# Moving the V products of an attention loop behind the next pair's first two products, with their copies and stores

## The reference, cut to what matters

```python
q = _rope((x @ wq).reshape(B, S, 32, 128)); k = _rope((x @ wk).reshape(B, S, 8, 128)); v = (x @ wv).reshape(B, S, 8, 128)
scores = einsum('bqhgd,bshd->bhgqs', qg, k) * sm_scale      # 64 x 64 per sequence and head, causal
attn = softmax(where(allowed, scores, min))
out = einsum('bhgqs,bshd->bqhgd', attn, v).reshape(B, S, 4096) @ wo
x = x + out
```

## Time and profile before

| | us |
|---|---|
| median of 3 runs | 2655.59 (2655.07 to 2657.83) |
| profiled execution | 2657.21 |
| its span in the trace | 2655.4 |
| PE matmuls busy | 2565.0 |
| DVE, POOL, ACT busy | 1672.6, 1442.6, 997.2 |

### The profile page before, as it was taken

The page is one execution under the profiler, slowest core; times in us unless marked ns, Lnnn a source line. Parts: engine busy times, 40 slices in busy tenths (PEclk is TensorE's granted clock), DMA queues, the critical chain, the costliest instruction groups (busy, mean ns, idle before and its releaser), DMA issues.

```text
span 2655.4 us, 37868 instructions
## 1 busy us (share of the span) xinstructions
PE 2565.0 (97%) x12584; PEld 2105.8 (79%) x12584; DVE 1672.6 (63%) x2357; ACT 997.2 (38%) x2440; POOL 1442.6 (54%) x1102
## 2 busy tenths in 40 slices
PE   8999899999998999999999989999999899999999
PEld 7778788888887788878877868888888678787887
DVE  3244566666776888864514456666677688886452
ACT  2043344444444444441204334444444444444120
POOL 0002777777777877730300277777777787773030
PEclk9999999999999999999999999999999999999999
DMA  3511222222225555413431112222222555541232
GB/s 135 174 61 59 68 84 105 104 88 88 104 88 191 178 171 162 140 36 86 133 128 64 60 58 94 105 98 94 88 104 85 186 182 175 159 139 40 78 103 75
DMA packets 150745, 289.96 MB, mean 109 GB/s; under 512 B 14706, under 2 KB 53746, under 8 KB 150562
## 3 DMA queue, kind: packets, MB, share of 16 engines
q1 hardware_dynamic: 105842, 212.08, 25.0%
q10 hardware_dynamic: 44720, 75.51, 7.7%
HBM read 213.41 MB, written 74.12 MB: 108 GB/s over the span
## 4 chain that ended last, share of the span: by engine, by line
PE 84%; POOL 9%; DVE 2%; ACT 2%; issue 1%; SPq 1%; DMA 0%; ACTq 0%; POOLq 0%; DVEq 0%
PE prod L800 26%; PE prod L802 25%; PE prod L801 25%; PE turned L964 4%; PE turned L989 2%; POOL slot L1806 2%; POOL slot_f L1801 2%; POOL s_f L1801 1%; POOL slot L1734 1%; PE turned L976 1%; POOL slot_f L1729 1%; PE turned L822 1%; ACT slot L1522 1%; PE turned L954 1%; DVE x_row L2237 0%
## 5 line engine op out<-in xcount | busy, mean ns | idle before, releaser
L800 PE MATMUL prod<-c_hi,slot 128*128 128x512 f32 x1280 | 510.3, 399 | 35.5 <-ACT p_sum L1560 21.4
L802 PE MATMUL prod<-c_hi,slot 128*128 128x512 f32 x1280 | 500.6, 391 | 0.0
L801 PE MATMUL prod<-c_lo,slot 128*128 128x512 f32 x1280 | 499.9, 391 | 0.0
L800 PE MATMUL prod<-t_hi,slot 128*128 128x512 f32 x960 | 389.7, 406 | 5.9 <-DVE x_row L2237 4.0
L802 PE MATMUL prod<-t_hi,slot 128*128 128x512 f32 x960 | 376.7, 392 | 0.0
L801 PE MATMUL prod<-t_lo,slot 128*128 128x512 f32 x960 | 375.2, 391 | 0.0
L800 PEld LDWEIGHTS prod<-c_hi,slot 128*128 128x128 f32 x1280 | 240.9, 188 | 98.0 <-issue 44.4
L800 PE MATMUL prod<-x_hi,w_hi 128*128 128x512 f32 x656 | 260.1, 396 | 24.2 <-DVE x_lo L1960 9.6
L802 PEld LDWEIGHTS prod<-c_hi,slot 128*128 128x128 f32 x1280 | 241.0, 188 | 51.5
L801 PEld LDWEIGHTS prod<-c_lo,slot 128*128 128x128 f32 x1280 | 241.3, 189 | 47.0
L1729 POOL TENSOR_TENSOR s_f<-raw,raw 128x512 f32<-128x512 f32 x24 | 30.9, 1286 | 454.8 <-DMA raw<-in_wv 454.8
(11 more groups left out here) (202 smaller groups left out, 4995.2 us busy)
## 6 DMA issues: line engine op xcount, KB each, us to landing
o_scratch<-o_f ACTq DMA_DIRECT2D x32, 1024.0 KB, 4.3
c_lo_f<-o_scratch SPq DMA_DIRECT2D x128, 256.0 KB, 3.1
t_lo_f<-o_scratch SPq DMA_DIRECT2D x96, 256.0 KB, 2.9
raw<-in_tw SPq DMA_DIRECT2D x34, 512.0 KB, 3.5
raw_a<-in_wq SPq DMA_DIRECT2D x32, 512.0 KB, 4.1
raw<-in_wq SPq DMA_DIRECT2D x32, 512.0 KB, 4.2
o_scratch<-o_f ACTq DMA_DIRECT2D x30, 512.0 KB, 2.8
raw<-in_wo SPq DMA_DIRECT2D x32, 384.0 KB, 4.2
```

The source lines that it names most:

```text
L800: pe.matmul(dst, wh, xh, start=start, stop=False, skip_group_check=skip)
L801: pe.matmul(dst, wh, xl, start=False, stop=False, skip_group_check=skip)
L802: return pe.matmul(dst, wl, xh, start=False, stop=stop, skip_group_check=skip)
```

## The change

V of a couple's first unit moves from position 6 to 7 (before P1 of the next pair, right ahead of the turn of the second unit's probabilities), V of the second unit from 8 to 9 (before P2 instead of P6; in Q01 pairs right ahead of the first turn of v). On ACT the store of the first unit follows into the next pair, behind `take_p(spill)`, and the store of the second unit stands behind the cast for P6 instead of the cast for P1. The tables for the first slot are changed in the same sense. The number of instructions is the same on every engine; POOL, DVE and SP keep their lists.

```diff
-PV_AT = (6, 8)
+PV_AT = (7, 9)
...
-                TAIL = {(0, P1): [(turn_p, 5)], (0, P6): [(pv, 5), (score, 6)], (0, P7): [(score, 7)],
+                TAIL = {(0, P1): [(pv, 4), (turn_p, 5)], (0, P6): [(score, 6)], (0, P2): [(pv, 5)], (0, P7): [(score, 7)],
...
                     if spill is not None:
                         take_p(B, spill)
+                        o_store(B, spill - 1)
...
-                    if spill is not None:
-                        o_store(B, spill)
                     if host is not None:
                         exp(B, host)
                     if not last:
@@ -1471,6 +1470,8 @@
                     else:
                         w_hi_b(0, P6)
                         o_hi(0, P1)
+                    if spill is not None:
+                        o_store(B, spill)
                     if lp % 3 == Q01:
                         take_v(B, lp // 3, 0)
...
-                    if host is not None:
-                        o_store(B, host)
                     if last:
                         o_hi(0, P7)
...
-                TAIL = {(0, 0): [(take_p, 5)], (0, 2): [(o_store, 5)], (0, 5): [(exp, 6)], (0, 9): [(exp, 7)],
+                TAIL = {(0, 0): [(take_p, 5), (o_store, 4)], (0, 3): [(o_store, 5)], (0, 5): [(exp, 6)], (0, 9): [(exp, 7)],
```

## The result

| | before | changed |
|---|---|---|
| median of the runs, us | 2656.4 (4 runs) | 2691.3 (4 runs) |
| ratio | | 1.013, 95% interval 1.0115 to 1.0145 |
| span of the profiled execution, us | 2655.4 | 2689.4 |

A forecast was written before the change was run, and what follows sets the result against it. PE, busy 97% of the span, was taken to bound the kernel. Merges of -0.3 us and waits of +6.3 gave +6.0, from 2655.6 to 2661.6 us; the 8 in 10 range was 2653 to 2667.

The forecast's parts named there:

- The term for PE's merges: On PE, V products placed right before turns save little switching: a gain of 0.3 us, bounds 3.5 loss and 4.2 gain.
- the bound if V left for nothing: PE leaves V before a turn at no cost: 4.2 us gain; as a rival without the wait, 2651.4 us, chance 0.06.
- a sign that it is wrong: On PE, merged stretches of V and turn coming out over 0.05 us shorter each would show the forecast wrong.
- The path of the wait: KV pair's store delays P2's cast and POOL's sum 1.10 us; Q01 pair's second V turn waits 0.45, 14 times: 6.3 us.
- The rest costs nothing: First unit's store at the next pair's start delays POOL about a microsecond, absorbed by waits and slack; output-stage passage hidden.
- the step before it: ACT and POOL in the KV pair: exponentials start when row_max arrives, unchanged; P2's cast comes 1.10 us late.
- The signs that were named: Some 14 more L954 waits for `v_tok` of 0.3 to 0.8 us; POOL's P2 residual about 1.1 us later in KV pairs.
- Rival C: In KV pairs the store's DMA is late too, moving POOL's chain another 0.27 us: 10.1 us loss, 2665.4; chance 0.09.
- The margin of 0.23 us: In the KV pair, the store's DMA lands at 414.15, before POOL reaches `parts` at 414.38: not late, by 0.23 us.
- Rival D: TensorE's clock falls at each new wait, 3.0 us in 14 places: 42 us, 2704 at most; chance 0.03.

The follow-up runs named there:

- second experiment: Changed kernel with the second unit's output store in KV pairs behind ScalarE's cast for P2 instead of ahead of it; 2697.8 us, ratio 1.0154.
- third experiment: Changed kernel with the store of the block parts (1024 KB) behind ScalarE's casts P7 and P4 in all pairs; 2726.4 us, ratio 1.0259.

## Why the prediction was wrong

**The term for PE's merges was ten times too small.** It gave them 0.3 us, by the row of a score behind V, with 4.2 us as the bound if V left for nothing. Measured on the float32r matmuls, they are worth 3.1 us, near that bound. V ahead of a turn keeps its 1.09 us, and the turn takes 0.41 us to the next product instead of 0.35, not 0.44; with the slow first matmul that a product has behind V gone, each merge is 0.08 us shorter. The prediction named over 0.05 us as a sign that it is wrong, and this sign came. So a merge saves something although the count of changes between 64 and 128 rows is the same, and the row of the score was not a stand-in for the turn. In the sum this error is small and points the other way: it does not explain the loss.

**The path of the wait was right, and so was its size without what I left out.** The cast for P2 was to be 1.10 us late, the last sum 1.10, the turn 0.45. In the kernel with the row step on ScalarE they are 0.98, 1.12 and 0.53 us, the wait comes in 13 places, and the time is 2662.8 where 2661.6 was forecast. In the changed kernel the three are 1.99, 2.59 and about 2.0 us. That the total with the row step on ScalarE is so near is in part luck: the merges take back 3.1 us where 0.3 was forecast, and the passages cost 3.1 (0.6 of it the thirteenth wait) where nothing was.

**The step that failed is "The rest costs nothing".** It let the first unit's store delay POOL by a microsecond, "which in the KV pair ends in its wait of 3.85 us", and the step before it took the start of the exponentials (407.42) as fixed, since DVE's work hangs on rotations that don't move. Both looked only at semaphores. POOL doesn't signal DVE there, yet DVE's step waits for POOL's instruction. The signs that were named came, with other sizes: 14 new entries at L954, but of 1.1 to 1.9 us and not 0.3 to 0.8, and the cast for P2 1.99 us late and not 1.1. The terms of the 1.49 us between 1.10 and 2.59: exponentials 0.71, a store that holds ACT for 1.98 and not 1.79 us (0.19), one more POOL instruction held up by DVE's normalisation of the probabilities (0.45: the sum at 421.70 takes 1.74, not 1.29), and 0.14 left over.

```profile
421.70 1.74 POOL L1728 TENSOR_TENSOR slot_f<-raw_a 128x512 f32<-128x512 f32 x1
```

It could have been read in the trace of before. There the scaling of row_max takes (ns: least, median, most) 171, 239, 1140, where its size never changes; in the changed kernel the median is 666:

```profile
L2093 DVE TENSOR_SCALAR row_max<-row_max x64: 171/239/1140, 310.8 to 2114.4; 128x8 f32<-128x8 f32 x64
```

```profile
L2092 DVE TENSOR_SCALAR row_max<-row_max x64: 171/666/1262, 310.4 to 2148.7; 128x8 f32<-128x8 f32 x64
```

**Rival C had a cause that exists, but not in the changed kernel.** It priced a late DMA for `parts` at 0.27 us. In the changed kernel `parts` never waits for one; in the second experiment, with the store one cast later, this wait was 1.73. The margin of 0.23 us on which it was put aside was thinner than the errors of the sum.

**Rival D was put too low, and half right.** The clock falls to half behind three of fourteen waits, at 1.6 us each, not 3.0 behind all. Between an idle time of 0.27 us (no fall) and one of 5.5 (fall) the rows of before had nothing, and I took the near one. For waits of the size that was forecast it was the right one: with the row step on ScalarE (gaps of 0.75 to 0.85 us) the granted clock stays at 1.00 behind all of them. Windows of 4 us behind the same wait, in the changed kernel and in the one with the parts late in Q01 pairs; the column behind POOL is the granted clock:

```profile
439.00:443.00 4.00, 4.00 (x14) 3.29 (x14) 0.93 (x2) 0.89 (x2) 3.62 (x3) 0.57 0.07 28
```

```profile
438.30:442.30 4.00, 4.00 (x21) 3.34 (x21) 0.98 (x2) 0.86 (x2) 3.65 (x3) 1.00 0.08 28
```

**The loop's end was in no step.** Its 6.0 us, taken to be the fetch of code behind a store's data, come from PE being later than the store. At the first border the fetch led the data by 0.8 us in before; in the changed kernel PE is 4.4 us later there, by its waits and the half clock, and the data 2.4, so that the fetch falls into them.

**Open:** why the clock falls behind three of the six pair 7 gaps of 2.2 us in the changed kernel and behind none of the six, 2.16 to 2.23, in the one with the parts late in Q01 pairs. The length of the gap alone doesn't decide it: in the third experiment, with gaps of 3.7 to 4.1 us, it fell behind eleven of twelve and stayed at 1.00 behind one of 3.71, while it fell behind all six of 2.4 to 2.9 us in the second. The passages cost 1.1 and 1.2 us with the copy first, 0.3 and 1.2 with their old order on top, and nothing with the KV pairs' store behind the casts as well; which moved store does that wasn't separated.

## What to carry to other kernels

When a step is moved into "idle time" of an engine, follow it past the semaphores: which instructions of the engine that it delays will now overlap others that share something with them. An instruction whose duration varies in the trace while its size doesn't is the sign of such a contact, and its least and most are the price list. A cost of changing between kinds of work is read from a row of the same neighbours: a score behind V said 0.01 us a merge, a turn behind V saves 0.08. And where several moves each eat from one slack, cost them together: here one half of the change was free, the other cost 6.5 us, and the two together cost 35.

## What the runs showed of the hardware

- DVE's TENSOR_SCALAR on 128 x 8 float32, in place, takes 0.17 us, or lasts until the POOL instruction under way ends: in 95 of 95 places with such an overlap in the two traces to within 0.06 us, and in 33 of 33 without one it took under 0.2. TENSOR_REDUCE (0.69 us always) is never held. The normalisation with two SBUF inputs takes 0.69 us alone and up to 1.8 beside POOL, and a POOL instruction that starts during it 1.74 and not 1.29.
- At a jump back to a loop's start PE goes on 2.6 to 3.2 us after one packet on the instruction queue (20 of 20 borders). Where the data of the 1024 KB store was already moving, the packet came only when it had ended (7 of 7). With the fetch ahead of the data the border costs 0.35 to 1.0 us, behind it 2.4 to 2.6. The list of waits names some other engine for it.
- Half clock (granted 0.50) behind gaps of PE at the second turn of V, in the loop turns of the changed kernel, the second experiment, the third and the one with the Q01 parts late: at gaps of 2.0 us or less in 0 of 12, at 2.15 to 2.25 in 3 of 18, at 2.4 to 2.9 in 6 of 6, at 3.7 to 4.1 in 11 of 12.
- V products (64 rows, float32) between float32r products make PE's stream 1.316 us longer standing alone, 1.286 right ahead of a score and 1.235 right ahead of a turn.
